# Score pair ahead of the burst and of the transposed scores in each attention unit

## The reference

```python
scores = jnp.einsum('bqhd,bkhd->bhqk', Q, K) / math.sqrt(HEAD_DIM)
alpha = jax.nn.softmax(scores, axis=-1)
alpha = jnp.where(causal, alpha, jnp.zeros((), dtype=alpha.dtype))
Y = jnp.einsum('bqhk,bkhd->bqhd', alpha, V).reshape(b, n, d)
...
x = x + _layernorm(_L0_attn_ref(_layernorm(x, axis=-1), ...), axis=-1)
x = x + _layernorm(_L0_ffn_ref(_layernorm(x, axis=-1), ...), axis=-1)
```

## Time and profile before

| | |
|---|---|
| median of 3 runs (lowest, highest) | 1539.58 us (1539.1, 1542.72) |
| profiled execution: its time, its span | 1539.73 us, 1537.8 us |
| busy over the span: PE, DVE, ACT, POOL | 92%, 60%, 52%, 40% |
| score pairs on PE (L1261) | 1024 matmuls of 379 ns as listed |
| reductions on DVE (L1699) | 512 of 1217 ns, 607.2 us |
| exponentials of chunks on ACT (L921) | 768 of 595 ns, 436.1 us |
| idle DVE ahead of L1699, for PE's score pair | 132.8 us |
| idle ACT ahead of L921, for PE's chunk | 157.0 us |

### The profile page before, as it was taken

The page is one execution under the profiler, slowest core; times in us unless marked ns, Lnnn a source line. Parts: engine busy times, 40 slices in busy tenths (PEclk is TensorE's granted clock), DMA queues, the critical chain, the costliest instruction groups (busy, mean ns, idle before and its releaser), DMA issues.

```text
span 1537.8 us, 28642 instructions
## 1 busy us (share of the span) xinstructions
PE 1417.4 (92%) x9774; PEld 820.1 (53%) x9775; DVE 925.1 (60%) x1740; ACT 805.4 (52%) x1717; POOL 610.9 (40%) x729
## 2 busy tenths in 40 slices
PE   6788999999999999999999998899999999999990
PEld 3444233333333233323332333699999999999980
DVE  4587787777888988898889887861111111111115
ACT  4444777777777777777777787321111111111114
POOL 2234334443454445444544441433333333333325
PEclk9999999999999999999999999999999999999995
DMA  3665732022202331223114141656666666666646
GB/s 122 155 158 126 247 42 42 7 37 42 42 15 28 42 42 18 25 42 42 20 23 97 56 138 57 175 163 192 172 178 191 176 178 187 182 175 182 189 113 222
DMA packets 100405, 166.85 MB, mean 108 GB/s; under 512 B 12400, under 2 KB 67568, under 8 KB 100304
## 3 DMA queue, kind: packets, MB, share of 16 engines
q1 hardware_dynamic: 86192, 146.08, 35.8%
q0 software_dynamic: 13632, 18.69, 7.6%
q10 hardware_dynamic: 480, 0.79, 0.3%
HBM read 130.76 MB, written 34.77 MB: 108 GB/s over the span
## 4 chain that ended last, share of the span: by engine, by line
PE 68%; DVE 18%; issue 6%; ACT 5%; POOL 2%; DMA 2%; ACTq 0%; POOLq 0%; DVEq 0%
PE ps L1206 16%; PE ps L1220 15%; PE ps L1104 11%; DVE negmax L1699 10%; PE ps L1074 9%; PE ps L1261 8%; ACT wfc L921 2%; PE ps L1043 2%; PE ps L1067 2%; POOL wfc L833 1%; PE ps L1248 1%; DVE x L1517 1%; PE ps L1193 1%; DVE mv L1506 1%; PE ps L1052 1%
## 5 line engine op out<-in xcount | busy, mean ns | idle before, releaser
L1699 DVE TENSOR_REDUCE negmax<-ps 128x1 f32<-128x1024 f32 x512 | 607.2, 1217 | 134.3 <-PE ps L1261 132.8
L921 ACT ACTIVATE wfc<-ps 128x512 f32<-128x512 f32 x768 | 436.1, 595 | 162.7 <-PE ps L1074 157.0
L976 ACT ACTIVATE wfc<-ps 128x512 f32<-128x512 f32 x142 | 84.8, 597 | 420.9 <-PE ps L1206 420.9
L1206 PEld LDWEIGHTS ps<-yx,wfc 128*128 128x128 f32 x2272 | 264.3, 192 | 4.2 <-issue 0.9
L1206 PE MATMUL ps<-yx,wfc 128*128 128x128 f32 x2272 | 265.7, 275 | 0.2 <-issue 0.2
L765 POOL TENSOR_TENSOR wfc<-wfc,causal 128x512 f32<-128x512 f32 x128 | 162.3, 1268 | 241.3 <-issue 108.8
L1220 PE MATMUL ps<-arena,wfc 128*128 x1136 | 257.3, 379 | 0.9 <-DMA arena<-in_L_ffn_w_proj 0.7
L821 POOL DMA_INDIRECT expert_out<-wfc,rt x71 | 113.0, 1592 | 299.9 <-DVE wfc L1663 291.9
L1220 PEld LDWEIGHTS ps<-arena,wfc 128*128 128x128 f32 x1136 | 210.3, 190 | 27.2 <-issue 1.6
L1261 PE MATMUL ps<-arena 96*128 96x512 bf16 x704 | 211.6, 382 | 9.1 <-DMA arena<-qk_parts 5.7
L1074 PE MATMUL ps<-arena 120*128 120x512 bf16 x528 | 202.0, 390 | 11.9 <-ACT wfc L921 0.4
(11 more groups left out here) (208 smaller groups left out, 1259.3 us busy)
## 6 DMA issues: line engine op xcount, KB each, us to landing
wfc<-in_L_ffn_w_fc SPq DMA_DIRECT2D x71, 1024.0 KB, 5.3
arena<-qk_parts SPq DMA_DIRECT2D x126, 128.0 KB, 5.6
qk_parts<-x SPq DMA_DIRECT2D x32, 384.0 KB, 2.8
arena<-in_L_ffn_w_proj SPq DMA_DIRECT2D x8, 1024.0 KB, 8.3
wfc<-qk_parts SPq DMA_DIRECT2D x60, 128.0 KB, 5.8
expert_out<-rt SPq DMA_DIRECT2D x3, 1408.0 KB, 12.2
yx<-in_L_attn_content SPq DMA_DIRECT2D x8, 512.0 KB, 4.3
x<-in_L_attn_content SPq DMA_DIRECT2D x1, 4096.0 KB, 14.0
```

The source lines that it names most:

```text
L921: nc.scalar.activation(et_sb[b % NET][:, hl, :], bk(ebank(c, g)), ACT.Exp).then_inc(s_expB, 1)
L976: nc.scalar.activation(hidT[s][:, 4 * hf:4 * hf + 4, :], bk(1 + hf).rearrange("p (c t) -> p c t", c=4), ACT.Gelu).then_inc(s_ge, 1)
L1206: ins = nc.tensor.matmul(bk(1 + hf)[:, c * P:(c + 1) * P], w1[s][:, kc * FF + (4 * hf + c) * P:kc * FF + (4 * hf + c + 1) * P], xsT[:, kc, :],
L1699: nc.vector.tensor_reduce(negmax[:, hl % 2, i:i + 1], ps[:, 2 * (k % 2):2 * (k % 2) + 2, :], AX.XY, ALU.max, negate=True).then_inc(s_max, 1)
```

## The change

In `body` of the tensor block the score pair moves up, ahead of the burst and of the first chunk. The turn back stays ahead of it, the maxima's transpose stays between it and the second chunk. The other engines' programs are the same, and so are the banks, the waits and every matmul.

```diff
                         ins.then_inc(s_T4, 1)
-                    pieces(p, u, k)
-                    todo = due(at_chunk, k)
-                    chunk(p, u, *todo[0])
                     if live(p, 0):
                         hl, i = divmod(k, QT)
...
                         for hf in range(2):
                             ins = nc.tensor.matmul(bk(2 * (k % 2) + hf), qs[u][0:SROWS, hl, i * P:(i + 1) * P],
                                                    ks[u][0:SROWS, hl, hf * 512:(hf + 1) * 512], start=True, stop=True)
                         ins.then_inc(s_S, 1)
+                    pieces(p, u, k)
+                    todo = due(at_chunk, k)
+                    chunk(p, u, *todo[0])
                     for hl, back in due(at_m, k):
```

## The result

| | before | change |
|---|---|---|
| median, us (lowest to highest) | 1539.72 (1539.1 to 1542.72) | 1569.97 (1568.63 to 1574.06) |
| ratio, 95% interval | | 1.0197 [1.0173, 1.0221] |
| span of the profiled execution, us | 1537.8 | 1572.1 |
| chain: PE, DVE, ACT, issue | 68, 18, 5, 6% | 64, 12, 11, 8% |

What follows compares the result with a forecast made beforehand. PE and ACT waiting for each other were taken to set the pace. 4.7 x 2.65 + 10 x 1.95 gave 32 us, 39 with small losses; 34 was taken, and 1539.7 + 34 = 1573.7 us, range 1557 to 1592.

Steps and rivals of the forecast that it cites:

- What bounds: Attention: PE and ACT wait for each other, DVE mostly behind; PE bounds burst units, ACT bounds between bursts.
- Units 5 to 8, +0.43: First stretch between bursts: the whole moved pair lands in the gap, next first chunk at 4.86 instead of 4.43 us.
- back-to-back exponentials 0.57 apart: Price for ACT, read from the timeline before: successive exponentials start 0.57 us apart.
- the walk: Step-by-step timing of PE and ACT through three kinds of stretch between bursts, at prices from the timeline; chance 84%.
- Units 8 to 10, +0.13: Second stretch between bursts: unit 9's second chunk starts earlier; +0.06 or +0.20 us by trace, +0.13 taken.
- Units 10 to 13, +0.32: Third stretch between bursts: first chunk behind the burst at 4.81 us instead of 4.49.
- The turn of unit 3: PE's turn in unit 3 fills time in which PE would wait: 0.15 us a group back.
- The turn of unit 13, -0.37: PE's turn no longer waits 0.52 us for DVE's copy: stretch 5.08 us instead of 5.45, 0.7 back a group.
- 2.65 us a group: Added per 32-unit group without layer norm: 3.5 less 0.7 and 0.15 for the turns; 50.25 becomes 52.9 us.
- 1.95 us a group: Added per group with layer norms: the period grows from 50.97 to 52.9 us, as without them.
- The 0.7 us that DVE adds should be covered: In layer norm groups DVE's extra 0.7 us should vanish: pairs come earlier, and 52.9 us is enough time.
- the pair waits for DVE at the head of the queue: Rival: a pair whose bank is held blocks burst and both chunks; 24 us in ten groups, 1598 us; chance 7%.

Runs made afterwards that it cites:

- ln_moved_after: The change with the layer norms' variance, its root and both scalings moved to other units on DVE and POOL: 1559.18 us, ratio to before 1.0129.
- ln_moved_chunk: Kernel before reordered to pair, first chunk, burst, second chunk in every unit, with layer norm steps moved to units 12, 14 and 16: 1554.53 us, ratio 1.0098.

## Why the prediction was right, and where its steps were off

The range held the time and the direction was the forecast one. By its steps:

- **What bounds.** PE and ACT wait for each other, and a burst unit is bound by PE: held. Of the orders of PE in the table, each with a pair between the chunks around a burst lost 26.8 us or more, and each without lost 0 to 7.
- **Units 5 to 8, +0.43.** Measured +0.28 (4.71 against 4.43). The gap behind the burst grew by 0.42, as walked. The size that was off is the price of ACT: "back-to-back exponentials 0.57 apart". It is the mean of two steps in the group of three at 338.03: about 0.65, where the second chunk came 0.66 behind the first and ACT had to wait for it, and 0.49. In the change both chunks are there, and the two start 0.49 apart (350.31 and 350.80). The last chunk before the next burst thus came 0.14 sooner (347.93, 2.76 behind the first, where the walk had 2.90).
- **Units 8 to 10, +0.13.** Measured +0.12 in three stretches of a group and -0.02 in the one of the earlier trace rows, where the change takes 3.64 against 3.66. The walk had 3.72, too long by the same price.
- **Units 10 to 13, +0.32.** Measured +0.23: 4.72 from 340.45 to 345.17, against 4.49. The turn of unit 3 was to bring this to +0.17; its stretch grew by 0.27.
- **The turn of unit 13, -0.37.** Measured -0.49. In the groups without layer norms it starts 2.98 behind the first chunk of unit 10 (walk: 3.07) and waits no more. With layer norms DVE's copy still holds it, 0.49 us, so PE's wait for L1710 fell only from 8.3 to 3.9 us.
- **2.65 us a group without layer norms.** Measured 1.74. By the starts of the first chunks behind all twelve bursts it is 1.15 in the four stretches of the first kind (walk 1.72), 0.35 in the second (0.52) and 0.24 in the third with both turns (0.43). So ACT's price accounts for nearly all of the difference.
- **1.95 us a group with layer norms.** Measured 2.22. The step that failed is "The 0.7 us that DVE adds should be covered". They add 1.2 us. The new order shifted DVE's layer norm steps against POOL's L744: L1506 grew from a median of 1.19 to 1.87 us and the second scaling from 1.06 to 1.95. ln_moved_after takes the 1.2 us back to nothing. The rival "the pair waits for DVE at the head of the queue" had the place right and a part of the mechanism: behind the second scaling the pair waits 0.34 us for L1699 (542.15 above), and that stretch is 0.51 longer than without layer norms. Its size was far off, 5 us in ten groups where it had 24, and the other 0.69 is the turn's wait for L1710.
- **The sum.** 34 us forecast and 30.3 measured. The walk was 4.7 x 0.91 = 4.3 us too high in one kind of group and 10 x 0.27 = 2.7 us too low in the other; the 2 us above the walk's 32 came on top. That the total is nearer than its parts is luck: the two errors have opposite signs. (In the prediction's larger sum, 3.1 a group makes 53.35 with layer norms, 2.38 more than 50.97, so ten groups give 23.8 and not 24.5.)
- **What was to be seen.** ACT's wait was to rise by some 40 us and rose by 43.9. The period was to be 52.9 in both kinds and was 51.99 and 53.19. The idle time behind a burst was to be 1.27 us and is mostly 1.04 to 1.36, with 0.81 at the shortest and 2.1 where DVE holds the turn. One sign did not come: DVE's own wait for the pair behind bursts was to go, and it still stands there, because the next unit's pair now comes behind the burst and two chunks:

```profile
346.24 3.77 DVE L1699 TENSOR_REDUCE negmax<-ps 128x1 f32<-128x1024 f32 x3 [0.90 <-PE ps L1258]
```

The rule of the Trainium skill that was weighed (Perfetto Trace Analysis, "Identifying the Most-Contended Engine") would have had the change gain by feeding DVE, the busiest engine. No gain came, but the change hardly fed DVE either: its wait for pairs fell only from 63.9 to 60.7 us. What speaks against taking DVE as the bottleneck is that DVE stayed at 79 and 89% busy while the time moved by 30 us with ACT's idle time. Only in the groups with layer norms did DVE set part of the pace, 0.7 us of 51 before.

## What to carry to other kernels

In a loop in which one engine (here PE) feeds two others, ask of every long step which of the others runs dry behind it. No other work belongs between that engine's last input ahead of the step and its first behind it: the same pair cost nothing in plain units and, between the chunks around a burst, 26.8 us or more. When several queues are shifted against each other, look again at the short instructions that grew longer, and at what another engine ran at that moment.

## What the runs showed of the hardware

**DVE instructions held for the length of a POOL instruction.** L1506 adds a constant to 2 elements a partition: 0.17 us alone, and 1.86 us when POOL's L744 of 1.90 us had started 0.06 us ahead of it. Started 0.73 us behind L744, it takes 1.19. L1517 (two inputs in SBUF, 128x256) goes from 0.48 to 2.20 us, L1521 (two inputs in SBUF, 128x2) from 0.15 to 1.88. Where L744 starts 0.36 us behind the DVE instruction, as in ln_moved_chunk, L1517 keeps its 0.48; at 0.01 us behind (472.30 and 472.31 above) it did not:

```profile
473.74 0.48 DVE L1517 SCALAR_TENSOR_TENSOR x<-yx,rstd,x 128x256 f32<-128x256 f32 x1
474.10 1.89 POOL L744 TENSOR_TENSOR arena<-mT,dmask 24x1024 bf16<-24x1024 bf16 x1 [1.07 <-ACT mT L905]
474.13 1.88 DVE L1521 TENSOR_TENSOR shift<-mv,rstd 128x2 f32<-128x2 f32 x1
```

The reductions from PSUM (L1699) hardly change: 1217 and 1220 ns on average. The Trainium skill, GPSIMD Engine Reference, "Specifications", says that GpSimd's SBUF interfaces are shared with VectorE and that there is contention with DVE instructions in a 2-port mode or with two SBUF inputs. For L1517 and L1521, with two inputs in SBUF, the traces agree, and show the size: the DVE instruction ends only when POOL's has. L1506 has one input, and no trace shows in which mode it runs.

**ACT's pace depends on what is ready.** Two exponentials of 512 columns start 0.49 us apart when both chunks are there (350.31 and 350.80, the chunks at 349.88 and 350.11). When ACT has run dry, an exponential starts 0.42 to 0.43 us behind the start of its chunk (342.45 behind 342.03, 350.31 behind 349.88).
